# First attention: values in two products with high and low halves side by side, and a moved step on VectorE

## The reference

```python
B, T, D = x.shape                      # 4, 256, 256
H, Dh = (16, 16)
q = (x @ Wq.T).reshape(B, T, H, Dh).transpose(0, 2, 1, 3)
k = (x @ Wk.T).reshape(B, T, H, Dh).transpose(0, 2, 1, 3)
v = (x @ Wv.T).reshape(B, T, H, Dh).transpose(0, 2, 1, 3)
scores = jnp.einsum('bhqd,bhkd->bhqk', q, k) * scale
causal = jnp.tril(jnp.ones((T, T), dtype=bool))
scores = jnp.where(causal, scores, -jnp.inf)
attn = jax.nn.softmax(scores, axis=-1)
out = jnp.einsum('bhqk,bhkd->bhqd', attn, v)
out = out.transpose(0, 2, 1, 3).reshape(B, T, D)
return out @ Wo.T
```

## Time and profile before

| | us |
|---|---|
| executions | 936.19, 939.78, 939.19 |
| median | 939.19 |
| the profiled execution | 939.04 |
| its span in the profile | 937.1 |
| outside the span | 1.9 |

### The profile page before, as it was taken

How to read it: one execution, slowest core, us unless ns; L and a number is a source line. 1 busy time by engine, 2 the same in 40 slices (tenths; PEclk the granted TensorE clock), 3 DMA queues, 4 the chain that set the end, 5 groups by cost and what they waited for, 6 DMA issues and landing times. The chain is left out here.

```text
span 937.1 us, 18767 instructions
## 1 busy us (share of the span) xinstructions
PE 863.4 (92%) x6108; PEld 799.0 (85%) x6108; DVE 616.3 (66%) x1620; ACT 567.0 (61%) x1570; POOL 456.4 (49%) x486
## 2 busy tenths in 40 slices
PE   5799997769999999999999999969999999999994
PEld 4699987668989989999889999858888888888884
DVE  5466768667787788877887777664545545454456
ACT  6889888656767776667676676654334343333333
POOL 3734334277677776677677777610222212222121
PEclk9999999998999999999999999997999999999997
DMA  7000000051124111411111111101433333333321
GB/s 238 1 22 27 22 23 1 23 147 35 34 61 122 47 40 40 136 46 45 36 35 46 45 37 47 41 1 41 150 107 102 116 117 100 112 101 117 118 79 45
DMA packets 50246, 63.34 MB, mean 68 GB/s; under 512 B 5728, under 2 KB 36064, under 8 KB 50176
## 3 DMA queue, kind: packets, MB, share of 16 engines
q1 hardware_dynamic: 49088, 61.41, 22.4%
q10 hardware_dynamic: 1088, 1.05, 0.3%
HBM read 41.86 MB, written 1.18 MB: 46 GB/s over the span
## 5 line engine op out<-in xcount | busy, mean ns | idle before, releaser
L639 POOL TENSOR_TENSOR b_prob<-b_prob,b_rsum 128x256 f32<-128x256 f32 (+1 forms) x128 | 104.8, 840 | 104.3 <-DVE b_rsum L621 104.3
L73 PE MATMUL banks<-act_t,b_w 128*128 128x256 f32 (+1 forms) x392 | 129.5, 330 | 4.4 <-DVE b_work L1203 3.3
L74 PE MATMUL banks<-act_t,b_w 128*128 128x256 f32 (+1 forms) x392 | 127.4, 325 | 0.0
L75 PE MATMUL banks<-act_t,b_w 128*128 128x256 f32 (+1 forms) x392 | 127.1, 324 | 0.0
L1965 ACT ACTIVATE moe_hid<-banks 128x512 fp32r<-128x512 f32 x66 | 39.5, 598 | 124.6 <-DVE banks L2056 124.6
L1364 ACT ACTIVATE b_prob<-banks,b_negmax 128x128 f32<-128x128 f32 (+1 forms) x256 | 103.6, 416 | 12.6 <-DVE b_negmax L1351 12.5
L2049 DVE TENSOR_TENSOR moe_gated<-banks,moe_share 128x512 f32<-128x512 f32 x66 | 45.6, 691 | 85.1 <-PE banks L75 81.2
L1220 ACT ACTIVATE b_qt<-b_work 128x512 fp32r<-128x512 f32 x64 | 40.5, 632 | 97.5 <-POOL b_work L1215 97.5
L1215 POOL TENSOR_TENSOR b_work<-b_work 128x512 f32<-128x512 f32 x64 | 88.1, 1377 | 9.2
L639 POOL TENSOR_TENSOR a_prob<-a_prob,a_rsum 128x256 f32<-128x256 f32 x64 | 52.4, 840 | 75.5 <-DVE a_rsum L621 75.3
L1211 POOL TENSOR_TENSOR b_work<-b_work,rope_t 128x512 f32<-128x512 f32 x64 | 83.2, 1299 | 7.2 <-DMA b_work<-b_work 7.2
(11 more groups left out here) (237 smaller groups left out, 3019.1 us busy)
## 6 DMA issues: line engine op xcount, KB each, us to landing
b_work<-b_work SPq DMA_DIRECT2D x128, 128.0 KB, 2.3
moe_share<-gates SPq DMA_DIRECT2D x32, 512.0 KB, 3.6
b_w_raw<-in_b_wq SPq DMA_DIRECT2D x4, 1024.0 KB, 5.5
b_w_raw<-in_b_wo SPq DMA_DIRECT2D x4, 1024.0 KB, 9.0
a_src_t<-act_t SPq DMA_DIRECT2D x5, 512.0 KB, 3.0
moe_w_raw<-in_wg SPq DMA_DIRECT2D x16, 128.0 KB, 2.1
moe_w_raw<-in_wu SPq DMA_DIRECT2D x16, 128.0 KB, 2.2
moe_w_raw<-in_wd SPq DMA_DIRECT2D x16, 128.0 KB, 2.2
```

Of the source, the lines that this page charges most:

```text
L73: nc.tensor.matmul(out, w_lo, m_hi, start=start, stop=False, skip_group_check=skip)
L74: nc.tensor.matmul(out, w_hi, m_lo, start=False, stop=False, skip_group_check=skip)
L75: return nc.tensor.matmul(out, w_hi, m_hi, start=False, stop=stop, skip_group_check=skip)
L639: last = self.m.nc.gpsimd.tensor_tensor(rows, rows, rsum[:, :, t:t + 1].to_broadcast([PART, 2, width]), ALU.mult)
```

## The change

1. **Values in two products.** The high and the low half of a head's v stand side by side in one weight tile: 32 columns for each head, 16 high and 16 low, four heads in 128 columns. One weight tile is multiplied by the low half and by the high half of the probabilities. `o_ps` therefore has two groups of four heads, 128 rows by 512 columns in all, and its rows hold a high and a low partial result of each head. (The product of both low halves is now included.)
2. **The projection adds them.** `wo` is a copy of the output weights in which the rows of a head stand twice, below each other, for its high and low partial results. It is made by 16 DMAs on SyncE's queue at the start of the stage (`sp_spread`), in front of the loads of `src_t`. The projection now runs over the two groups: twelve matmuls in place of six. `act_outputs` and `dve_outputs` copy 512 columns in place of 256.
3. **VectorE's order.** AttentionA has its own `slot_dve`: maxima of head 1, the low half of the probabilities, maxima of head 2, and the rest as before.
4. GpSimd's clearing of v covers half as much, as there is one tile in place of two.

```diff
+    def slot_dve(self, dve, it, p, units=True):
+        now = self.stage(it, p, 0)
+        if now:
+            self.dve_max(dve, *now[1:], heads=(0,))
+        if prob := self.stage(it, p, 3):
+            self.dve_prob_t(dve, *prob[1:])
+        if now:
+            self.dve_max(dve, *now[1:], heads=(1,))
+        if before := self.stage(it, p, 1):
+            self.dve_normalise(dve, *before[1:])
...
-        self.v = place(2 * NTT * HPI * PART, "p (a t h n) -> p a t h n", a=2, t=NTT, h=HPI)
+        self.v = place(NTT * HPI * PART, "p (t h n) -> p t h n", t=NTT, h=HPI)
...
-        self.ot = sb("ot", [PART, 2, SEQ], F32R)
+        self.ot = sb("ot", [PART, 2, VG * SEQ], F32R)
+        self.wo = place(2 * NC * VG * D, "p (a c g n) -> p a c g n", a=2, c=NC, g=VG)
...
+        if isinstance(it, int) and it == 0 and p == PAIRS - 1:
+            wait(pe, self.wo_spread, 16 * SPREADS)
...
-                last = three(nc, m.o_ps[:, k * PART:SEQ],
-                             self.v[:, 0, k, head, :], self.v[:, 1, k, head, :],
-                             self.prob_t[:, par, 0, at:at + width], self.prob_t[:, par, 1, at:at + width],
-                             head == 0 and k == 0, head == HPI - 1 and k == NTT - 1)
+                g = head // VH
+                for part in (1, 0):
+                    last = nc.tensor.matmul(m.o_ps[:, g * SEQ + k * PART:(g + 1) * SEQ], self.v[:, k, head, :],
+                                            self.prob_t[:, par, part, at:at + width],
+                                            start=head == 0 and k == 0 and part == 1,
+                                            stop=head == HPI - 1 and k == NTT - 1 and part == 0,
+                                            skip_group_check=True)
...
+    def sp_spread(self, sp):
+        src = self.m.a_wo[:].rearrange("p (a c n) -> p a c n", a=2, c=NC).bitcast(F32)
+        for g in range(VG):
+            for h in range(VH):
+                of = (g * VH + h) * A_DH
+                for part in range(2):
+                    to = (2 * h + part) * A_DH
+                    sp.dma_start(self.wo[to:to + A_DH, :, :, g, :].bitcast(F32), src[of:of + A_DH, :, :, :],
+                                 ).then_inc(self.wo_spread, 16)
...
-            last = three(nc, m.y_ps[:, t * D:(t + 1) * D],
-                         self.ot[:, 0, t * PART:(t + 1) * PART], self.ot[:, 1, t * PART:(t + 1) * PART],
-                         m.a_wo[:, bass.ds(at, D)], m.a_wo[:, bass.ds(at + NC * D, D)], True, True)
+            for g in range(VG):
+                o = lambda part: self.ot[:, part, g * SEQ + t * PART:g * SEQ + (t + 1) * PART]
+                last = three(nc, m.y_ps[:, t * D:(t + 1) * D], o(0), o(1), self.wo_at(it, 0, g),
+                             self.wo_at(it, 1, g), g == 0, g == VG - 1)
...
-        self.m.nc.scalar.activation(self.ot[:, 0, :], self.m.o_ps[:, 0:SEQ],
+        self.m.nc.scalar.activation(self.ot[:, 0, :], self.m.o_ps[:],
...
-        self.m.nc.vector.tensor_tensor(self.ot[:, 1, :], self.m.o_ps[:, 0:SEQ],
+        self.m.nc.vector.tensor_tensor(self.ot[:, 1, :], self.m.o_ps[:],
```

More of the change, by code:

```diff
@@ L318, in _ @@
             nc.gpsimd.memset(m.q_stack[:, 0:NTT * HPI * PART].bitcast(F32), 0.0)
-            k_at = 2 * B_W + 2 * NTT * HPI * PART
+            k_at = 2 * B_W + NTT * HPI * PART
             nc.gpsimd.memset(m.b_w[:, k_at:k_at + NTT * HPI * STACK].bitcast(F32), 0.0)
@@ L603, in slot_act, with dve_max @@
             self.act_weights(act, it)
-    def dve_max(self, dve, p, P):
+    def dve_max(self, dve, p, P, heads=(0, 1)):
         nc, m = self.m.nc, self.m
         wait(dve, self.exp_done, 2 * P - 2)
-        for h in range(2):
+        for h in heads:
             wait(dve, self.s_full, 2 * P + 1 + h)
@@ L705, in run @@
                 after(k)
+VH, VG, SPREADS = 4, 2, 16
 class AttentionA(Attention):
+    def slot_dve(self, dve, it, p, units=True):
[8 more added lines that the diff above has]
+            self.dve_normalise(dve, *before[1:])
+        if out := self.stage(it, p, 4):
+            self.dve_outputs(dve, *out)
+        u = self.early_unit(p, units)
+        if u is not None:
+            self.dve_unit(dve, it + 1, u)
+        if now and p == PAIRS - 1:
+            self.dve_values(dve, it)
+        if p == 0 and not (isinstance(it, int) and it < 2):
+            self.dve_add(dve, it - 2)
     ITS, UNITS = A_ITS, 4
@@ L877, in v_view @@
     def v_view(self, part, t):
-        base = self.v[:, part, t, 0, 0:A_DH]
+        base = self.v[:, t, 0, part * A_DH:(part + 1) * A_DH]
         return bass.AP(tensor=base.tensor, offset=base.offset,
-                       ap=[list(base.ap[0]), [PART + A_DH, HPI], [1, A_DH]])
+                       ap=[list(base.ap[0]), [VH * PART, VG], [PART + 2 * A_DH, VH], [1, A_DH]])
     def act_values(self, act, it):
@@ L888, in act_values @@
         for t in range(NTT):
-            row = self.values(it, t).rearrange("p (h d) -> p h d", h=HPI)
+            row = self.values(it, t).rearrange("p (g h d) -> p g h d", g=VG, h=VH)
             last = nc.scalar.activation(self.v_view(0, t), row, ACT.Copy)
@@ L962, in _ @@
         def _(sp):
+            self.sp_spread(sp)
             def load(it, b):
@@ L973, in _ @@
             sp.wait_ge(self.src_loaded, 16 * (self.ITS - self.COPIED))
+            sp.wait_ge(self.wo_spread, 16 * SPREADS)
         @block.gpsimd
```

7 lines of the change are left out of this document (5 added, 2 removed).

## The result

The changed kernel took 948.98 us (median of 6 executions, 946.24 to 953.62) against 939.49 us for the kernel before on the same chip. The ratio is 1.0122, with an interval of 1.0103 to 1.0141. On the 939.19 us of before that ratio is 950.7 us: the direction was right, the rise was 11.5 us where 8.4 was forecast, and it ends 0.2 us above the upper end of the range. (The two medians by themselves are 9.5 us apart, a ratio of 1.0101; the six times of the changed kernel lie in two groups, 946.2 to 946.9 and 951.1 to 953.6.)

The account below looks back on a forecast made before the run. TensorE was taken as the bound before, a ScalarE-VectorE chain around the iteration after. Five iterations +5.5, ramp 0, last slots +1.95, drain +0.95: +8.4 on 939.04 gives 947.5 us, range 938.5 to 950.5.

Parts of the forecast that it names:

- What bounds: Attention A, 60 to 125 us: TensorE bounds before; after, a ScalarE-VectorE chain makes an iteration 17.65 us instead of 16.48.
- the moved step: VectorE's low half between both heads' maxima: head 2's exponentials start at least 1.39 us after head 1's, 0.6 late.
- The rival that TensorE stays the bound: Attention A: iteration 15.33 us, TensorE's eight waits shrink by 0.53 each, total 930 us; chance 0.13.
- The chain around it: ScalarE and VectorE steps followed from slot 1's scores around one attention A iteration, next slot 1 at 17.68, taken as 17.65.
- The cancelling rival: Slots 2 and 3 absorb the late start, only slots 0 and 1 pay 0.6: iteration 16.5, total 939 us; chance 0.16.
- The matmuls: TensorE in attention A: a pair's values fall from 1.40 to 0.93 us, the projection grows from 0.80 to 1.52.
- Five iterations: Saturated stretch of attention A: five times 1.17 us, less 0.35 in the first, +5.5 us.
- End of the stage: Attention A's last six slots with scores through the last outputs +1.95 us, and its drain +0.95 us.
- The copied weights at nothing: Start of attention A: sixteen 64 KB DMAs issue in 23 us on SyncE's queue, done by about 45, costing 0.
- "Attention B starts behind a barrier and just moves": Everything behind attention A was taken to start later but keep its length: no change.

Follow-up runs that it names:

- the values alone: Changed kernel with VectorE's old order, so only values, copies and projection differ from the kernel before: 942.90 us, ratio 1.0052.
- the second profile: The unaltered changed kernel profiled once more; that execution took 947.96 us, and the run measured 949.58 us, ratio 1.0120.
- the run with filled waits: Changed kernel plus seven unread transposes on TensorE in each of six late slots, in front of the probability transposes: 949.05 us, ratio 1.0122.
- the first profile: The profiled execution of the changed kernel in its main measurement, the longest of the six: 953.62 us, span 951.8.

## Why the prediction was right and wrong

**What bounds, and the moved step: right.** The rival that TensorE stays the bound fell as the second head's exponentials came 1.39 us behind the first's, the number of the forecast. An iteration was forecast at 17.65 and took 17.58, and the steps of the chain in between came within 0.03 us of their forecast places. The chain around it was confirmed from the side by moving the addition: one VectorE step of 0.60 less on it made each iteration shorter by 0.6. Taken alone, its halves were forecast less well (16.6 and 16.96 against 16.85 and 17.14). And TensorE stands idle for less than the 2.3 us of the forecast: its busy time leaves (65 - 60.37) / 65 of 17.58, or 1.25 us an iteration; busy times of matmuls overlap at their ends, so this is a lower bound. The cancelling rival expected slots 2 and 3 to absorb the late start; but with the new order in those slots alone the iteration was still 17.00, longer than the 16.85 without it.
The Trainium skill ("Perfetto Trace Analysis", section on the most-contended engine) says to begin with the engine of highest occupancy, and to judge TensorE's headroom by its weight loads and its useful work and not by matmul busy time. TensorE was that engine by both busy times, 65.00 of 65 us for matmuls and 63.28 for weight loads. Its work was cut, and the runs show a loss, also with the values alone (16.85 us against 16.48): here the rule names the engine, and not whether the time saved can be passed on by the two that hand work around.

**The matmuls: right in sum, one reading wrong.** Projection 1.53 us (forecast 1.52), the values of a pair 0.86 (0.93). That the 128-column matmuls are not cheaper was misread. In the kernel before, three of 256 columns take 0.44 us from start to start (114.56 to 115.00) and three of 128 columns 0.28 (115.00 to 115.28), and over all pairs from 60 to 125 us the means are 0.139 and 0.094 each. The 0.117 is the mean of both widths, and no pace of 128-column matmuls; it served here because the change takes out one in three of each width.

**Five iterations: right.** They cost 87.71 - 82.32 = +5.4 (forecast +5.5).

**End of the stage: right in its sum in one profile, and partly by luck.** All that follows up to attention B cost 50.94 - 48.01 = +2.9 in the second profile, as forecast (1.95 + 0.95). Divided at the end of VectorE's output copy in the last slot with scores, it is 2.3 and 0.6. And the second profile already has some of the lower clock in it: the slot of 5.80 us took 4.99 with the clock up, so about 0.8 of the 2.9 was not waiting or work as forecast (an estimate from the run with filled waits, since its transposes stand in that slot too). In the first profile the same stretch is another 2.1 longer, with more of it at the lower clock. That TensorE's longer idle time in the last slots would be followed by a lower clock, which the kernel before has nowhere from 130 to 175 us, was missing in these two terms.

**The copied weights at nothing: right, by a wrong size.** The 16 issues took 10.5 us (18.83 to 29.3), 0.65 each, where I had 23 from 1.45 each, and no value product waited for them. The row was misread: its 7.24 us go from the first of the five issues to the end of the last, with pauses between pairs of them. One issue takes 0.46 to 0.60 us, as a pair of the same DMAs later in attention B shows, two issues in 1.10 us:

```profile
208.10 1.10 SPq L1191 DMA_DIRECT2D b_work<-b_work  x2
```

**"Attention B starts behind a barrier and just moves": this step failed.** It was sized at 0 for all 759 us behind the barrier, with no range at all. It measured +1.4 in the second profile and +6.0 in the first. Of that, 3.0 (1.4 and 1.6 among the experts; 3.3 in the first profile) is shown: a piece of program was fetched just when the gates went out, moving the piece away takes the loss off the changed kernel, and moving it there puts the same loss on the kernel before without the change. That the piece moved because the change took matmuls out of TensorE's program is my reading of queue 8. The other part, -1.6 us in the second profile and +2.7 in the first, lies between attention B's first matmul and the gates' issue. That stretch is 473.6 us before, 476.3 and 472.0 in the two profiles of the changed kernel, and 470.7 to 474.1 in the other profiles of kernels without the change. So the same kernel varies there by more than the change could be seen to do; what decides it stays open. As a mean of the two profiles, attention A is 9.3 us longer and the rest 3.7, with 1.1 less before the first slot 1: most of what the forecast lacks lies in the rest, and the remainder in the lower clock at the end of attention A.

**The range.** Its upper end came from uncertainties of attention A alone. With 3 us for the rest it would have been 953.5, and would have held the result. The second profile, by itself, is not far from the forecast: 8.25 for attention A, 1.4 for the rest, 0.6 less before the first slot 1, that is 937.1 + 9.1 = 946.2.

## What to carry to other kernels

Before a step is moved between two releases in an in-order queue, count who waits for the second one: here an engine at 65% occupancy had the whole pipeline behind 0.86 us of its work, and relieving the engine at 100% gained nothing by itself. A change of the number of instructions can shift the times at which pieces of the program are fetched, so a stage that the change does not touch can lose or gain (here 3 us); look for an "instruction" row in the DMA view where a landing is late, and allow for it in a range. And compare two profiles of the same kernel before explaining a difference between two kernels.

## What the hardware showed that I had not expected

- A 16 KB piece of program on its DMA queue, started 1.0 us behind the issue of a 128 KB transfer, went with a landing after 3.3 to 4.0 us in place of 1.9, in seven profiles (0.8 to 1.1 us behind). Started 1.78 us behind, it did nothing (2.0). Four matmuls more in the kernel before are enough to go from the second case to the first.
- An idle time of TensorE that grew from 1.08 to 2.86 us was followed by 4 us at a mean granted clock of 0.57, which cost 1.6 us. At the same place an idle time of 2.43 us was not followed by a lower clock, and one of 2.50 us was.
- Sixteen 64 KB copies inside SBUF were issued in 10.5 us, 0.65 each.
- With TensorE busy or idle for 11.9 us at the end of attention A, the rest behind it took 757.1 and 758.7 us, neither more than before's 759.1.
